# An adaLN transformer block in split fp32: one modulation product, GpSimd's order of slots, the last unit and the last products are put in another order

## The reference

```python
mod = (_silu(L0_c) @ L0_wmod).reshape(L0_c.shape[0], 6, 1, -1)
sa, ca, ga, sb, cb, gb = (mod[:, i] for i in range(6))
ga = (2 * (ga >= 0) - 1) * jnp.maximum(jnp.abs(ga), 0.25)
gb = (2 * (gb >= 0) - 1) * jnp.maximum(jnp.abs(gb), 0.25)
h = _layernorm(x) * (1 + ca) + sa
# attention: q = h wq, k = h wk, v = h wv; rotary embedding on q and k;
# causal softmax of q k^T / sqrt(128); times v; times wo
x = x + ga * attention(h)
h = _layernorm(x) * (1 + cb) + sb
# gated MLP: x12 = h w12^T + b12; silu(x1) * x2; times w3^T, plus b3
x = x + gb * mlp(h)
```

## Time and profile before

| | |
|---|---|
| time, median of 3 runs | 797.05 us (796.18 to 797.47) |
| the profiled execution | 796.75 us, of which 795.0 us are the span of the trace |
| PE busy | 764.7 us (96%), granted clock 0.993 |
| DVE, ACT, POOL busy | 607.7 (76%), 506.9 (64%), 568.3 us (71%) |
| DMA | 147.13 MB, mean 185 GB/s |

### The profile page before, as it was taken

The page is one execution under the profiler, slowest core; times in us unless marked ns, Lnnn a source line. Parts: engine busy times, 40 slices in busy tenths (PEclk is TensorE's granted clock), DMA queues, the critical chain, the costliest instruction groups (busy, mean ns, idle before and its releaser), DMA issues.

```text
span 795.0 us, 11524 instructions
## 1 busy us (share of the span) xinstructions
PE 764.7 (96%) x3526; PEld 620.7 (78%) x3526; DVE 607.7 (76%) x1296; ACT 506.9 (64%) x1201; POOL 568.3 (71%) x384
## 2 busy tenths in 40 slices
PE   7989999999999999999999999999999998979997
PEld 2764788887888788888888888888888877767885
DVE  6866888777877787778778787878687788459685
ACT  2726676766676767676677667777677765955331
POOL 1644786879577957795769677898778998447453
PEclk9899999999999999999999999999999999999999
DMA  9625646775867676766776767866677855989011
GB/s 313 232 69 148 195 117 202 179 251 127 235 148 236 163 212 158 211 195 185 193 210 190 191 185 186 251 165 209 145 228 187 279 146 172 273 258 250 1 54 53
DMA packets 189782, 147.13 MB, mean 185 GB/s; under 512 B 60565, under 2 KB 166165, under 8 KB 187673
## 3 DMA queue, kind: packets, MB, share of 16 engines
q1 hardware_dynamic: 189304, 146.33, 65.0%
q10 hardware_dynamic: 416, 0.07, 0.0%
HBM read 91.82 MB, written 54.53 MB: 184 GB/s over the span
## 4 chain that ended last, share of the span: by engine, by line
PE 50%; POOL 23%; ACT 10%; DVE 10%; issue 4%; DMA 3%; SPq 0%; DVEq 0%; ACTq 0%; POOLq 0%
PE q_bank L511 12%; PE out_bank L602 10%; POOL pT_lo L1422 8%; PE o_bank L579 7%; PE x_bank L511 7%; PE s_bank L511 5%; POOL rope_tmp L1448 5%; ACT probs L1192 4%; POOL wo_lo_sb L1422 3%; POOL qT L1422 3%; ACT probs L1200 3%; POOL wq_lo_sb L1422 2%; PE s_bank L802 1%; PE s_bank L789 1%; ACT pT_hi L1169 1%
## 5 line engine op out<-in xcount | busy, mean ns | idle before, releaser
L1422 POOL TENSOR_TENSOR pT_lo<-pT_raw,pT_hi 128x1024 fp32r<-128x1024 f32 (+1 forms) x96 | 194.2, 2038 | 60.5 <-ACT pT_hi L1169 60.5
L1192 ACT ACTIVATE probs<-probs,neg_max 128x32 f32<-128x32 f32 (+15 forms) x256 | 130.6, 512 | 147.8 <-DVE neg_max L864 147.8
L1422 POOL TENSOR_TENSOR qT<-rope_tmp,qT 128x512 fp32r<-128x512 f32 x64 | 83.0, 1296 | 83.0 <-ACT qT L1169 83.0
L882 DVE STREAM_TRANSPOSE turned<-probs 128x512 f32<-128x512 f32 (+1 forms) x64 | 96.7, 1511 | 33.7 <-DMA spread_dram<-turned 24.7
L1448 POOL TENSOR_TENSOR rope_tmp<-rope_tmp 128x512 f32<-128x512 f32 x80 | 110.7, 1390 | 14.4 <-DVE rope_tmp L829 14.4
L1200 ACT ACTIVATE probs<-probs,row_inv 128x32 f32<-128x32 f32 (+15 forms) x256 | 111.9, 508 | 1.8 <-DVE row_inv L872 1.8
L511 PE MATMUL q_bank<-hT_hi,wq_hi_sb 128*128 128x512 f32 x244 | 97.0, 397 | 5.0 <-DVE rope_tmp L829 4.9
L511 PE MATMUL s_bank<-k_both,qT 128*128 128x416 f32 (+11 forms) x576 | 99.4, 321 | 1.8 <-DVE neg_max L864 1.8
L602 PE MATMUL out_bank<-wo_hi_sb,attn_hi 128*128 128x512 f32 x248 | 97.6, 393 | 1.6 <-DVE attn_lo L886 1.2
L864 DVE CUSTOM_DVE_ANT_0 probs<-s_bank,mask_sb 128x416 f32<-128x416 f32 (+2 forms) x192 | 87.1, 501 | 14.1 <-PE s_bank L511 13.9
L602 PE MATMUL out_bank<-wo_hi_sb,attn_lo 128*128 128x512 f32 x248 | 97.3, 392 | 0.0
(11 more groups left out here) (265 smaller groups left out, 1683.7 us busy)
## 6 DMA issues: line engine op xcount, KB each, us to landing
spread_dram<-turned SPq DMA_DIRECT2D x64, 256.0 KB, 3.8
pT_raw<-spread_dram SPq DMA_DIRECT2D x16, 1024.0 KB, 5.9
spread_dram<-turned SPq DMA_DIRECT2D x64, 192.0 KB, 3.8
pT_raw<-spread_dram SPq DMA_DIRECT2D x16, 768.0 KB, 4.9
wq_raw<-in_L_attn_wq_dram SPq DMA_DIRECT2D x36, 256.0 KB, 4.2
wo_raw<-in_L_attn_wo_dram SPq DMA_DIRECT2D x9, 1024.0 KB, 5.5
...
```

What stands on the lines that cost most here:

```text
L882: nc.vector.transpose(dst, src).then_inc(blocks_turned, 1)
L1192: nc.scalar.activation(rows, rows, ACT.Exp, bias=neg_max[:, par, t:t + 1], scale=-1.0, accum_out=row_sum[:, par, t:t + 1]).then_inc(exp_do ...
L1422: nc.gpsimd.tensor_tensor(dst, src, hi.bitcast(f32), ALU.subtract).then_inc(done, 1)
```

## The change

Six edits, all in the order of work; no product is added or removed.

- PE: `modulation_rows(4)` stands right behind `modulation_rows(3)`, ahead of the group loop; `turn_rows(3)` and `turn_rows(4)` follow the first scores. The row of modulation 5 goes to `f_blocks` instead of `f_raw`, and `gate_rows` waits for `mod_made` 4 for both gates.
- POOL: in groups 1 to 5, what `later` holds (`f_low`, `wq_low`, `wv_low`) of slots 0 and 4 moves into the next slot, behind `q_low` and `k_low`.
- POOL: `wq_low` of the first group waits for `norm_ready` 2.
- Last group and `last_unit`: another order on PE, DVE and ACT; `project_out(g, 0)` goes to `q_bank`; the norm of sequence 0 moves from ACT to DVE as `tensor_scalar`.
- SP: `load_w12(2)` stands behind the stores of slot 5.
- PE: the end of `down(1, ...)` takes row tiles 0 and 1 through chunks 2 and 3 first, then tiles 2 and 3.

```diff
@@ PE @@
+                if not (isinstance(g, int) and g == 0 and s == 0):
                     need(pe, roped, ROPE_GROUP, g, ROPE_FIRST + rope_q_at(s) - (1 if s % TT == 1 else 0))
...
                     if first and s == 0:
-                        pe.wait_ge(roped, 5)
+
+                        turn_rows(3)
+                        turn_rows(4)
                         project_q(out_bank[:, :], 1, 0, h_lo[1])
-                    if first and s == 1:
-                        pe.wait_ge(roped, ROPE_FIRST)
-                        modulation_rows(4)
                     if first and s == 2:
-                        turn_rows(4)
                         modulation_rows(2)
...
                 scores(g, 4)
-                project_out(g, 0)
+
+                project_out(g, 0, dst=q_bank, added=-1)
                 attend(g, 1)
 
                 scores(g, 5)
                 attend(g, 2)
+                project_out(g, 1)
+
+                scores(g, 6)
                 pe.wait_ge(v_turned, B * KV)
+                need(pe, wo_added, SLOTS, g, 1)
                 turn_x1(0, (0, 1))
-                project_out(g, 1)
-                turn_x1(0, (2, 3))
-
-                scores(g, 6)
-                up(0, 0)
                 attend(g, 3)
                 project_out(g, 2)
+                turn_x1(0, (2, 3))
 
                 scores(g, 7)
                 project_out(g, 3)
+                up(0, 0)
                 attend(g, 4)
                 up(0, 1)
...
             pe.wait_ge(roped, 4)
             modulation_rows(3)
+            pe.wait_ge(roped, 5)
+            modulation_rows(4)
...
-            down(1, ([0, 1], [2], [3]))
+            down(1, ([0, 1],))
+            down(1, ([2],), range(2))
+            down(1, ([3],), range(2))
+            down(1, ([2, 3],), range(2, TT))
@@ DVE, last_unit @@
                 maxima(g, 4)
+                add_out(g, 0, src=q_bank)
+                invert(g, 4)
+                attn_low(g, 1)
                 norm_scale(0, B + 1)
-                attn_low(g, 1)
-                add_out(g, 0)
-                invert(g, 4)
+
+                maxima(g, 5)
+                norm_x1(0)
                 turn_blocks(g, 4)
                 attn_low(g, 2)
-
-                maxima(g, 5)
-                for k in range(KC):
+                v_low(g, 1, 2)
+                add_out(g, 1)
+                invert(g, 5)
+
+                maxima(g, 6)
+                for k in range(2):
                     h2_low(0, k)
-                invert(g, 5)
-                add_out(g, 1)
-                v_low(g, 1, 2)
+                attn_low(g, 3)
+                add_out(g, 2)
                 turn_blocks(g, 5)
@@ ACT, last_unit @@
                 probs_high(g, 2)
+                exponents(g, 4)
                 attn_high(g, 1)
-                norm_x1(0)
-                exponents(g, 4)
                 normalise(g, 4)
                 attn_high(g, 2)
+                v_high(g, 1, 2)
+                probs_high(g, 3)
+
+                exponents(g, 5)
                 modulate_x1(0, (0, 1))
-
+                normalise(g, 5)
+                attn_high(g, 3)
                 modulate_x1(0, (2, 3))
@@ POOL @@
                     q_low(g, s - 1)
                     if r == 1:
                         k_low(g, s - 1)
+                        if stalls(g):
+                            later(g, s - 1)
...
+                    if r != 0 or not stalls(g):
+                        later(g, s)
+
+            def stalls(g):
+
+                return 0 < g < KV - 2 if isinstance(g, int) else True
+
+            def later(g, s):
+
+                if f_row_at(g, s - 1) is not None:
+                    f_low(f_row_at(g, s - 1))
+                w = (SLOTS * g + s + SLOTS - 1) // TT
+                if fresh(w):
+                    wq_low(LOAD[w], (s - 1) % TT)
+                    if s % TT == 2:
+                        wk_low(LOAD[w])
+                    if s % TT == 0:
+                        wv_low(LOAD[w])
...
             wk_low(0)
+            pool.wait_ge(norm_ready, 2)
             for h in range(REP):
                 wq_low(0, h)
```

More of the change, by code:

```diff
@@ L222, in adaln_block @@
         mod_banks = [q_bank, out_bank, out_bank, q_bank, out_bank, x_bank]
-        mod_row = [rope_tmp[0:B, 0, 0, :], rope_tmp[0:B, 0, 1, :], f_raw[0:B, :], f_raw[0:B, :], f_raw[0:B, :], f_blocks[0:B, :]]
+        mod_row = [rope_tmp[0:B, 0, 0, :], rope_tmp[0:B, 0, 1, :], f_raw[0:B, :], f_raw[0:B, :], f_blocks[0:B, :], f_blocks[0:B, :]]
         h_tmp = [[p_flat[1][:, k * T:(k + 1) * T] for k in range(KC)], [turned_flat[:, k * T:(k + 1) * T] for k in range(KC)]]
@@ L465, in group @@
                         load_w12(s - TT)
-                    if s == 5 and last:
-                        load_w12(2)
                     if s == 4 and last:
@@ L473, in group @@
                     blocks_to_dram(g, s)
+                    if s == 5 and last:
+                        load_w12(2)
                     if makes_v(g, s):
@@ L540, in slot_query @@
                 v, h = (SLOTS * g + s + 5) // TT, (s + 5) % TT
-                if isinstance(g, int) and g == 0 and s == 0:
-                    pe.wait_ge(mod_ready, 2)
-                    turn_rows(3)
-                else:
+                if not (isinstance(g, int) and g == 0 and s == 0):
                     need(pe, roped, ROPE_GROUP, g, ROPE_FIRST + rope_q_at(s) - (1 if s % TT == 1 else 0))
@@ L636, in group @@
                         project_v(batch_of(v))
-                    if s == 3 and last:
-                        project_out(g, s - 4)
                     if first and s == 3:
@@ L642, in group @@
                         attend(g, s - 3)
-                    if s != 3 and not (first and s < 4):
+                    if (s != 3 or last) and not (first and s < 4):
                         project_out(g, s - 4)
@@ L791, in up, with down @@
                     last.then_inc(up_made, 1)
-            def down(b, parts):
+            def down(b, parts, rows=range(TT)):
                 for ms in parts:
@@ L798, in down @@
                         pe.wait_ge(x4_made, 3)
-                    for i in range(TT):
+                    for i in rows:
                         for m in ms:
@@ L914, in group @@
                     r = s % TT
-                    if last and s == 3:
-                        add_x1(2)
                     maxima(g, s)
@@ L927, in group @@
                     if last and s == 3:
-                        x1_stats(0)
+                        add_x1(2)
+                        attn_low(g, 0)
                     invert(g, s)
@@ L933, in group @@
                     if last and s == 3:
-                        x1_stats(1)
-                        x1_stats(2)
+                        for n in range(2):
+                            x1_stats(n)
                         add_x1(3)
-                        attn_low(g, 0)
-                        x1_stats(3)
+                        for n in range(2, TT):
+                            x1_stats(n)
                     else:
@@ L960, in last_unit @@
                 maxima(g, 4)
+                add_out(g, 0, src=q_bank)
+                invert(g, 4)
+                attn_low(g, 1)
                 norm_scale(0, B + 1)
-                attn_low(g, 1)
-                add_out(g, 0)
-                invert(g, 4)
+                maxima(g, 5)
+                norm_x1(0)
                 turn_blocks(g, 4)
                 attn_low(g, 2)
-                maxima(g, 5)
-                for k in range(KC):
+                v_low(g, 1, 2)
[3 more added lines that the diff above has]
+                for k in range(2):
                     h2_low(0, k)
-                invert(g, 5)
-                add_out(g, 1)
-                v_low(g, 1, 2)
+                attn_low(g, 3)
+                add_out(g, 2)
                 turn_blocks(g, 5)
-                attn_low(g, 3)
-                maxima(g, 6)
-                add_out(g, 2)
                 invert(g, 6)
                 maxima(g, 7)
+                for k in range(2, KC):
+                    h2_low(0, k)
                 turn_blocks(g, 6)
@@ L1006, in last_unit, with norm_x1 @@
                 finish(0)
+            def norm_x1(b):
+                dve.wait_ge(norm_ready, B + b + 1)
+                dve.wait_ge(rope_lo, ROPE_GROUP * KV)
+                for w in range(TT * b, TT * (b + 1)):
+                    nc.vector.tensor_scalar(xn2[:, w % TT, :], acc[:, w, :], moments[:, w, 0:1], rstd[:, w, :],
+                                            ALU.subtract, ALU.mult).then_inc(x1_normed, 1)
             def moments_of(b, done):
@@ L1246, in norm_x1 @@
                 act.wait_ge(norm_ready, B + b + 1)
[L1247 to L1250 removed]
+                act.wait_ge(h2_turned, KC)
                 for w in range(TT * b, TT * (b + 1)):
@@ L1259, in group @@
                         q_high(g, s - 1)
+                        attn_high(g, 0)
                     exponents(g, s)
```

(14 more changed lines are left out.)

18 lines of the change are left out of this document (1 added, 17 removed).

## The result

The changed kernel takes 805.29 us (median of 5 runs, 803.53 to 807.48) against 797.05 us (796.18 to 797.57): a ratio of 1.0099, 95% interval 1.0085 to 1.0113. It is 8.2 us slower, where I had forecast 2.7 us less. The profiled execution took 805.83 us, with a span of 804.0 us.

What follows compares the result with a forecast made beforehand. PE was taken to bound the kernel from 100 to 600 us, other engines at the start, last unit and end. 796.75 - 2.4 + 0 + 3.0 - 2.0 - 1.3 = 794.05, plus 0.3 for the median: 794.4 us, range 788.5 to 801.

Steps and rivals of the forecast that it cites:

- rival 2: SP's queue, groups 1 to 5: probabilities queue behind the stores of `f`, another 1.3 us a group, 800.9 us; 21%.
- B: GpSimd's new order in groups 1 to 5: +0.6 us a group, +3.0 in all, range -5.2 to +10.
- B's own wait: Slot 6's q product, groups 1 to 5: waits for the moved `wq_lo`, so the stall grows from 1.05 to 1.65 us.
- Rival 1: Groups 1 to 5: the stall at slot 6 goes and none replaces it, -5.2 us, 786.2 in all; 15%.
- A: Start: the fifth modulation fills PE's idle stretch ahead of the first scores, -2.4 us, range -2.4 to -1.0.
- The norm's wait: Start: GpSimd's `wq_lo` behind `norm_ready` only moves VectorE's held microsecond to another instruction; 0, range -1.0 to +0.3 us.
- C: Last group and unit: slot 5's transpose starts earlier, so `attend(5)` does too; -2.0 us, range -2.6 to +2.
- D: The end: row tiles 0 and 1 finish early, so the last add ends sooner; -1.3 us, range -1.6 to -0.4.

Runs made afterwards that it cites:

- f_kept: The changed kernel with `f_low` alone back at its old place, `wq_low` and `wv_low` still moved: 789.12 us, ratio 0.9898.
- wv_moved: The changed kernel with only `wv_low` moved behind `q_low` and `k_low`, `f_low` and `wq_low` at their old places: 788.18 us, ratio 0.9884.
- a_only: The kernel before with only the fifth modulation moved ahead of the first scores: 795.06 us, ratio 0.9978.
- last_unit_only: The kernel before with only the last group's and last unit's new order and the new place of `load_w12(2)`: 796.78 us, ratio 1.0001.
- b_undone: The changed kernel with GpSimd's order in groups 1 to 5 put back as it was: 792.61 us, ratio 0.9940.

## Why the prediction was wrong

**The step that failed** is that the sum holds nothing for the stores of `f`. The text had their delay of 2 to 3 us and wrote: "If that reaches the path, each group loses another 1 to 1.4 us (a rival, below)". It took the idle time ahead of VectorE's transpose and PE's lead of three slots as cover, and gave rival 2 21%. The delay reached the path in all five groups. The transpose's idle time did not swallow it (5.31 us instead of 1.89), and PE's lead over `attend` was no cover, since, as the rows of group 4 show, the row maxima behind the transpose carry the delay, through ScalarE's and GpSimd's orders, to `wo_lo`, which PE wants one slot later. In the changed kernel slots 3 to 5 lost 8.6 us by it, 1.3 to 1.95 a group, where the sum had 0. Rival 2's place, the row maxima, was right, and its price of 1.3 was near the 1.7 that is the mean of the five groups. Where `f_low` alone is moved the stores cost 3.6 us a group by the medians, since a second place comes in, in slot 7, that the text had nowhere. With B at the measured +13.1 my own sum would have been 796.75 - 2.4 + 13.1 - 2.0 - 1.3 = 804.15, 804.5 by the median: the other terms did not matter for the verdict.

**B's own wait** was right in its place, and in its size in three of five groups: the same `wq_lo`, 1.57 to 1.79 us in groups 1, 3 and 4, for which I had 1.65. In groups 2 and 5 it was 0.36 and 0.35: there GpSimd had started `qT` 3.3 us ahead of the scores of slot 6 instead of 1.9 to 2.1. Why it was ahead there is not shown; PE had waited for `wo_lo` in all five. Slot 6 so lost 4.4 us in all where I had +3.0, and about 1.1 of them without the half clock: that +3.0 is near the sum is partly luck. In f_kept and wv_moved, without the stores, the arithmetic of the slot held to 0.5 us: the 2.7 us in which GpSimd waits for `qT` have room for two of the three operations. Rival 1's condition, "1.6 us to spare that I do not see", is what wv_moved makes true.

**The half clock** was missing from the bounds of B. The prediction's price of a stall was its length; in two of five places it was its length and 1.6 us more, 3.3 of the 13.1 us of this execution.

**A** was -2.4 and measured -2.1 (a_only -2.1, ratio 0.9978). The order at the start is as forecast: `rows(4)` at 45.99 and the scores at 49.52, no idle ahead of them. It was 0.3 us short.

**The norm's wait** was 0, and measured 0.4 with an interval that holds 0. In the changed kernel's trace the `newton` step fell from 1.18 to 0.16 us and the first `hT_hi` came at 19.41 instead of 21.02, of which 0.58 is that this execution's chain began earlier. But, as the prediction had it, the `hT_lo` behind it took 1.65 us, where it took 0.69, and the second cast was only 0.65 us earlier, nearly all of it the same 0.58. VectorE's held microsecond moved from one instruction to another. That follows from the rule of the Trainium skill (SBUF — State Buffer, "SBUF: two separate sides") that the two engines shut each other out for a whole instruction; the trace agrees, with 0.69 to 1.65 us for the same instruction. The other long row of the prediction, at 16.92, lies beside `wk_lo` and is 1.19 us long in the changed kernel too; it has a single input, so the case of two inputs that the prediction names does not cover it.

**C** was -2.0 and is -0.65 in the trace, nothing in last_unit_only. The mis-sized part is the 11.7 us that I took as fixed: it became 14.1 in b_undone with the 1 MB load in between, which the text had named among what stands against.

**D** was -1.3 and measured -1.4. The last rows of the trace, answering to the earlier trace rows:

```profile
800.68 0.77 DVE L1168 TENSOR_TENSOR acc<-acc,y_tmp 128x512 f32<-128x512 f32 x1
...
798.00 2.89 POOL L1540 TENSOR_TENSOR acc<-acc,y_tmp 128x512 f32<-128x512 f32 x2 [3.30 <-DVE y_tmp L1163]
```

The last add takes 0.77 us instead of 1.66, and GpSimd's sums end at 800.9, 0.2 behind the start of VectorE's last add.
